# Two expert blocks in plain fp32 instead of four, weights split in halves, tables built inside the whole blocks

## The chip, the cores and the metric

The kernel runs on one core of one Trainium2 chip. The metric is the device time of one execution in microseconds (us). The engines are named as in the profile: PE is the matmul engine, PEld its weight loads, ACT is ScalarE, DVE is VectorE, POOL is GpSimd, SP is SyncE. A name with a q behind it (SPq, ACTq) is that engine's instruction queue, from which transfers are issued.

## The reference

Sixteen images of 5 x 128 x 128 become 16 x 256 tokens of 256 features; then one attention layer with a decay, then a mixture of eight experts of which each token takes two. All of it is fp32.

```
h = layernorm(patches(x) @ W) * gamma                    # tokens: 320 -> 256
xn = layernorm(h)
q, k, v, g = silu(xn Wq), silu(xn Wk), xn Wv, sigmoid(xn Wg)   # 256 -> 1024, 16 heads of 64
cum = cumsum(-softplus(xn Wa + ba))                      # one per head and token
attn = (q k^T) * exp(cum_i - cum_j), causal
h += (groupnorm(attn v) * gn_w + gn_b) * g @ Wo
xf = layernorm(h);  p = softmax(xf Wr);  the two best experts of each token
h += sum over the two of p_e * (gelu(xf W1_e + b1_e) W2_e + b2_e)      # 256 -> 1024 -> 256
```

## The kernel before

**Parts of a product.** Most products are made from fp32 numbers cut in two: ACT copies the number into an fp32r tile (the high part, `*_hi`), DVE subtracts this from the number (the low part, `*_lo`), and PE adds three products, high by high, high by low and low by high (`three`). Some products are made from the plain fp32 numbers, without the cut; PE's records then have two instructions for each product.

**Attention.** It runs over eight pairs of images (p = 0 to 7), each in eight steps (c = 0 to 7), every engine with its own program, written out and ordered by hand; semaphores join them. A step makes queries, keys and gates of two heads, scores and the weighted sum. Ahead of the first step, SP loads the tokens' patches and the four attention weights (`load_weight`, L470), ACT and DVE cut them (`weight_hi` L856, `weight_lo` L1797), a fifth weight (wo) and the token weights (`token_weights_hi`, `token_weights_lo`) are cut within steps 0 and 1. The running sums `cum` go out to memory and come back spread over the partitions (`store_cum`, `load_decay`).

**Routing.** After attention, tokens are normed, their two experts chosen (`choose`, `weigh`, `keep_ranks`, `place` on DVE; `top_exp` on ACT; `route`, `ranks` on PE), and POOL scatters each token's row to its experts' lists (`scatter`).

**Expert blocks.** 256 rows of one expert's list are a block. Blocks 0 to 9 come from the counts of the first five pairs; their experts and places are in the table `tab` before attention ends (`first_tables`, `first_places`). The later blocks' places need the counts of all pairs; `last_tables` (L2022) makes them in 40 small DVE instructions, each of which waits for the one before. Of these, instruction 2 gives the ends of the lists (`padi`), to which SP writes padding (`pad_list`), instructions 39 and 40 write the table of blocks 10 and up.

The first NF = 4 blocks are **early** ones: plain fp32 (`early1`, `early2` on PE, `active_early` on ACT), put between the last steps of attention and of routing. Then come **whole** blocks, cut in parts, 4 to 21, in a loop of two blocks per pass (`whole_row` on PE L1673, ACT L1132, DVE L2298), and behind them **mixed** rounds with blocks of 128 rows. All engines take their work strictly in the order of their programs.

**The order in a whole row for block k.** PE: second half of layer 1 of k, transposes of the rows of k+1 (L1399), first half of layer 2 of k, first half of layer 1 of k+1, second half of layer 2 of k. ACT, for each of eight chunks c: the gelu of chunk c+1 (L964), the high part of the hidden chunk c (L984), and a quarter of the high part of the next block's w1 (c = 0 to 3) or w2 (c = 4 to 7) (L958); after c = 3 the high part of the next rows (L950). DVE, for each c: low part of the hidden chunk (L2123), a quarter of the low part of w1 or w2 (L2114), at c = 2 the block's result before (`keep_y`, L2091), at c = 3 the low part of the next rows, at c = 4 `row_tails`. ACT's first gelu of row k+1 waits for DVE's last hidden chunk of row k; PE's chunk c waits for the gelu four chunks before it (`hidden_free`).

**SP's order.** For each whole block: w1, w2, then b2 of the block before, the rows, b1 (`load_whole`, L586). Before block NF+2 stands `sp.wait_ge(M["tb"], 2)` (L644), before block 10 `sp.wait_ge(M["tb"], 40)` (L652); `tb` counts the table instructions. These lines:

```
            sp.wait_ge(M["tb"], 2)
            for j in range(NF + 2, N1):
                load_whole(whole(j), whole(j - 1))
                for e in range(X // 2):
                    pad_list(X // 2 * (j % 2) + e) if j < NF + 4 else None
            ...
            sp.wait_ge(M["tb"], 40)
            load_whole(whole(N1), whole(N1 - 1))
```

Of the kernel before, what the change touches and what calls it, by code (L numbers as in the profile page):

```python
# [27 lines left out]
P = 128  # L28
# [27 lines left out]
WQ = 4  # L56
YB = (BS + 1) // 2
HB = 4
NF = 4
# [16 lines left out]
def vit_layer(nc, xT, w_tok, gamma, wq, wk, wv, wg, wa, ba, wo, gn_w, gn_b,  # L76
# [3 lines left out]
    with ExitStack() as ctx:  # L80
# [224 lines left out]
        passed mh_done zeroed c_in c_sum ws_in0 ws_in1 ws_in2 ws_in3 ws_hi ws_lo wt_in g_in  # L305
        xt_in0 xt_in1 xt_in2 xt_in xth_done xtl_done wth_done wtl_done tok_ps s1_st s1_u s1_v0 s1_v1 s1_st2 s1_ve s1_rs s1_h s1_xn
        s1_tps s1_xnT s1_aps s1_z h_out sp_step sp_m sp_la gnh
        xh_done xl_done cum_ps cc_done ncum_done ct_ps ct_copied cum_out0 cum_out1
# [47 lines left out]
        def two_whole(q):  # L356

            return (Blk(2 * q, 0, q, 2 * q - NF, 4 * q, 4 * q - 2, q - 1, q - 1),
                    Blk(2 * q + 1, 1, q, 2 * q + 1 - NF, 4 * q + 2, 4 * q, q - 1, q - 1))

# [18 lines left out]
        W_IN = [("ws_in0", 1), ("ws_in1", 1), ("ws_in2", 1), ("ws_in3", 1), ("ws_in1", 2)]  # L379
        w_parts = [wsp[0], wsp[2], wsp[1], wsp[3], wo_sp]  # L380


        @block.sync
        def _(sp):
# [85 lines left out]
            def load_weight(i):  # L470
                have(sp, "ws_lo", 2 if i == 4 else 0)
                sp.dma_start(stage_w[i].rearrange("p (k n) -> p k n", k=EC if i < 4 else NP),
                             W_ATT[i].rearrange("(k p) n -> p k n", p=P)).then_inc(M[W_IN[i][0]], 16)
# [15 lines left out]
            store_h(1)  # L489
            load_weight(4)  # L490
# [7 lines left out]
            for p in range(NPR):  # L498
                for c in range(NP):
# [301 lines left out]
        def _(act):  # L801
            act.dma_start(wt[:, 0:KT, :], w_tok[0:KT * P, :].rearrange("(k p) n -> p k n", p=P)).then_inc(M["wt_in"], 16)
            for at in (0, KREM):
                act.dma_start(wt[at:at + KREM, KT, :], w_tok[KT * P:FEAT, :]).then_inc(M["wt_in"], 16)
            for dst, src in ((gammaB[:, :], gamma.rearrange("(a n) -> a n", a=1).broadcast_to([P, E])),
# [3 lines left out]
                act.dma_start(dst, src).then_inc(M["c_in"], 16)  # L809

# [13 lines left out]
            def token_weights_hi():  # L824
                act.wait_ge(M["wt_in"], 48)
                act.activation(wt_hi, wt[:, :, :], ACT.Copy).then_inc(M["wth_done"], 1)

            def softplus(p):

                act.wait_ge(M["s1_z"], p + 1)  # L830
# [25 lines left out]
            def weight_hi(i):  # L856
                act.wait_ge(M[W_IN[i][0]], 16 * W_IN[i][1])
                act.activation(w_parts[i][0].rearrange("p k n -> p (k n)"), stage_w[i], ACT.Copy).then_inc(M["ws_hi"], 1)
# [11 lines left out]
            def tanh_g(p, c):  # L870
                act.wait_ge(M["g_ps"], NP * p + c + 1)
                if p == 0 and c == GC:
                    act.wait_ge(M["ws_lo"], 5)
# [12 lines left out]
            def decay(p, c, u):  # L886
                n = 2 * NP * p + 2 * c + u
                act.wait_ge(M["causal"], 2 * (n + 1))
                act.wait_ge(M["ncum_done"], p + 1)
# [5 lines left out]
            def keep_o(p, c):  # L895
                act.wait_ge(M["o_ps"], 2 * NP * p + 2 * c + 2)
                have(act, "wo_ps", 4 * (p - 1) + 2 * (c // GC) + 2)
                act.activation(osb[:, c, :], bank[3][:, :], ACT.Copy).then_inc(M["o_done"], 1)
# [109 lines left out]
            def step(p, c):  # L1008
# [20 lines left out]
                if (p, c) == (0, 0):  # L1029
                    token_weights_hi()  # L1030
                if (p, c) == (0, 1):
                    weight_hi(4)
# [1385 lines left out]
```

## Time and profile before

| | |
|---|---|
| median of 3 runs | 1226.39 us (1219.59 to 1227.38) |
| the profiled execution | 1219.53 us, its span 1217.7 us, 1.8 us around it |
| busy share of the span | PE 98%, PEld 87%, ACT 71%, DVE 69%, POOL 35% |
| granted PE clock, mean | 0.997 |

Attention takes the span to about 740 us, the early blocks to about 820 us, whole blocks to about 1040 us, mixed rounds the rest. A row of a timeline gives start, duration, engine, line, operation, tiles and count; in brackets stands the engine's idle time before it and what ended that. Rows of one line and tile that follow each other are merged. A busy PE need not be PE at its peak, since its instructions overlap; the spacing of starts is the safer reading.

### The profile page before, as it was taken

The numbers are of one execution on the slowest core, as the hardware profiler recorded it, in microseconds if no ns is written. First come the engines' busy times: TensorE is split into PE (matmuls) and PEld (weight loads), VectorE is DVE, ScalarE is ACT, GpSimd is POOL, SyncE is SP. The second block draws the span as 40 slices with busy tenths as digits, with TensorE's granted clock in tenths as the row PEclk, the third lists the DMA queues.
The fourth block names the chain that finished last, engine by engine and source line by source line (L and its number), as shares of the span: only waits on it lengthen the run. The fifth ranks groups of instructions, "written<-read, shape, count | busy, mean of one in ns | idle before, by whom it ended". The sixth has DMA issues, their size and how long they took to land. (4 is left out here: it accounts for less than half of the span.)

```text
span 1217.7 us, 27487 instructions
## 1 busy us (share of the span) xinstructions
PE 1198.1 (98%) x8560; PEld 1055.2 (87%) x8560; DVE 844.5 (69%) x2182; ACT 868.7 (71%) x2033; POOL 429.7 (35%) x521
## 2 busy tenths in 40 slices
PE   9999999999999999999999999999999999999997
PEld 6788788788888888888888788889999999999996
DVE  5655676776776776776776677578888888465663
ACT  4767767767767767767767758458888888666663
POOL 2212222242242242242242151555454545443433
PEclk9999999999999999999999999999999999999999
DMA  6532232242242352342342248498988786899984
GB/s 201 180 112 83 91 108 92 89 144 87 94 144 82 99 144 81 100 144 81 100 127 85 95 125 274 144 279 238 266 227 247 218 247 184 238 290 255 277 248 99
DMA packets 126730, 195.39 MB, mean 160 GB/s; under 512 B 16497, under 2 KB 92625, under 8 KB 126481
## 3 DMA queue, kind: packets, MB, share of 16 engines
q1 hardware_dynamic: 111904, 176.22, 45.6%
q0 software_dynamic: 13584, 17.26, 7.2%
q8 instruction: 54, 0.88, 0.3%
q10 hardware_dynamic: 1136, 0.61, 0.2%
q14 instruction: 52, 0.42, 0.1%
HBM read 168.32 MB, written 29.05 MB: 162 GB/s over the span
## 5 line engine op out<-in xcount | busy, mean ns | idle before, releaser
L1276 PE MATMUL bank<-xn_sp,big_r 128*128 128x512 f32 x1152 | 297.1, 400 | 1.4 <-DVE dec_x L1822 0.9
L1276 PEld LDWEIGHTS bank<-xn_sp,big_r 128*128 128x128 f32 x1152 | 208.9, 189 | 48.1 <-issue 1.8
L700 POOL TENSOR_SCALAR_AFFINE_SELECT dec_x<-dec_x 128x256 f32<-128x256 f32 x256 | 112.2, 466 | 355.5 <-DMA dec_x<-cum_scratch 355.0
L893 ACT ACTIVATE dec_x<-dec_x,ncum 128x256 f32<-128x256 f32 (+1 forms) x512 | 186.7, 446 | 11.8 <-POOL dec_x L700 11.8
L1622 PE MATMUL bank<-big_r 128*128 128x256 f32 x1296 | 168.7, 286 | 1.0 <-ACT q_s L964 1.0
L1622 PEld LDWEIGHTS bank<-big_r 128*128 128x128 f32 x1296 | 161.0, 192 | 2.6 <-ACT q_s L964 1.6
L1822 DVE TENSOR_TENSOR dec_x<-bank,dec_x 128x384 f32<-128x384 f32 x256 | 125.5, 549 | 39.3 <-PE bank L1321 34.2
L757 POOL DMA_INDIRECT out<-mid_f,tok x68 | 116.4, 1711 | 63.6 <-DMA out<-mid_f,tok 26.7
L751 POOL TENSOR_SCALAR mid_f<-mid_f,dec_x 128x256 f32<-128x256 f32 x68 | 72.8, 1076 | 155.4 <-DVE mid_f L2091 152.9
L964 ACT ACTIVATE mid_f<-bank,h 128x256 f32<-128x256 f32 x216 | 101.1, 479 | 28.1 <-PE bank L1622 14.8
L2123 DVE TENSOR_TENSOR big_r<-mid_f,big_r 128x256 fp32r<-128x256 f32 x216 | 91.2, 423 | 38.0 <-ACT big_r L984 38.0
L2114 DVE TENSOR_TENSOR big_r<-big_f,big_r 128x512 fp32r<-128x512 f32 x148 | 101.4, 691 | 9.8 <-ACT big_r L958 2.6
L1269 PE MATMUL bank<-big_r,xn_sp 128*128 128x512 f32 x384 | 99.3, 395 | 0.3 <-ACT big_f L875 0.3
L1362 PE MATMUL bank<-big_r,y_sp 128*128 128x256 f32 x512 | 96.8, 284 | 0.0
L958 ACT ACTIVATE big_r<-big_f 128x512 fp32r<-128x512 f32 x148 | 93.7, 637 | 3.9 <-DMA big_f<-in_L_ffn_w 3.9
L984 ACT ACTIVATE big_r<-mid_f 128x256 fp32r<-128x256 f32 x216 | 92.1, 427 | 0.0
L1318 PE MATMUL bank<-q_s,k_s 64*128 64x256 f32 x512 | 83.8, 402 | 3.4 <-issue 3.0
L1634 PE MATMUL bank<-big_r 128*128 128x256 f32 x672 | 86.3, 285 | 0.0
L722 POOL DMA_INDIRECT expert_rows<-xn,slot x64 | 65.1, 1018 | 58.3 <-DVE slot L1965 42.2
L1269 PEld LDWEIGHTS bank<-big_r,xn_sp 128*128 128x128 f32 x384 | 70.7, 188 | 15.5 <-issue 1.4
L1634 PEld LDWEIGHTS bank<-big_r 128*128 128x128 f32 x672 | 82.2, 191 | 0.0
L1362 PEld LDWEIGHTS bank<-big_r,y_sp 128*128 128x128 f32 x512 | 81.2, 191 | 1.0
(257 smaller groups left out, 2327.4 us busy)
## 6 DMA issues: line engine op xcount, KB each, us to landing
big_f<-in_L_ffn_w SPq DMA_DIRECT2D x68, 1024.0 KB, 6.8
dec_x<-cum_scratch SPq DMA_DIRECT2D x128, 384.0 KB, 3.9
big_w<-in_L_ffn_w SPq DMA_DIRECT2D x12, 1024.0 KB, 7.7
mid_f<-expert_rows SPq DMA_DIRECT2D x27, 261.0 KB, 3.1
h_scratch<-h SPq DMA_DIRECT2D x16, 256.0 KB, 2.2
h<-h_scratch SPq DMA_DIRECT2D x8, 512.0 KB, 4.0
out<-h SPq DMA_DIRECT2D x16, 256.0 KB, 4.3
xt<-in_x SPq DMA_DIRECT2D x14, 256.0 KB, 4.3
```

The costliest lines, as they stand in the source:

```text
L700: pool.affine_select(out=d, in_=d, pattern=[[0, 2], [1, P]], compare_op=ALU.is_ge, fill=fill, base=0, channel_multiplier=-1).then_inc(M["c ...
L757: pool.indirect_dma_start(out=out_rows, out_offset=bass.IndirectOffsetOnAxis(ap=tok[k.par][:, s:s + 1], axis=0), in_=yo[k.par][:, s, :], i ...
L893: act.activation(d, d, ACT.Exp, bias=ncum[p % 2][:, NS * u + s, 2 * c + hh:2 * c + hh + 1]).then_inc(M["exp_done"], 1)
L958: act.activation(parts[0].rearrange("p k n -> p (k n)")[:, cols], staged[:, cols], ACT.Copy).then_inc(M[f"{name}_hi"], 1)
L964: act.activation(target, bank[hbank[c % HB]][:, 0:width], ACT.Gelu_apprx_tanh, bias=b1_sb[k.par][:, c:c + 1]).then_inc(M["gel_done"], 1)
L1269: mm = pe.matmul(bank[target][:, :], xp[:, k, t * P:(t + 1) * P], wp[:, k, n * 512:(n + 1) * 512], start=(k == 0 and j == 0), stop=(k == E ...
L1276: mm = pe.matmul(bank[target][:, :], wp[:, k, c * P:(c + 1) * P], xp[:, k, :], start=(k == 0 and j == 0), stop=(k == EC - 1 and j == 2))
L1362: mm = pe.matmul(bank[target][:, s * E:(s + 1) * E], yp[:, j, u * S + s * P:u * S + (s + 1) * P], wp[:, GC * g + j, :], start=(j == 0 and ...
L1622: mm = pe.matmul(bank[hbank[c % HB]][:, 0:BLK], wp[:, i, c * P:(c + 1) * P], xp[:, i, :], start=(i == 0 and j == 0), stop=(i == EC - 1 and ...
L1634: mm = pe.matmul(bank[6][:, s * E:(s + 1) * E], gp[:, c, s * P:(s + 1) * P], wp[:, c, :], start=(c == 0 and s == 0 and j == 0), stop=(c == ...
L1822: dve.tensor_tensor(d, score_bank(p, c, u, hh)[:, 0:LW], d, ALU.mult).then_inc(M["mult_done"], 1)
L2114: dve.tensor_tensor(lo, staged[:, cols], f32(hi), ALU.subtract).then_inc(M[f"{name}_lo"], 1)
```

## The change

NF becomes 2: blocks 2 and 3 become whole blocks. `last_tables` is cut into seven parts, `tables_0` to `tables_6`, which DVE does at c = 5 of the rows of blocks 2 to 8; DVE's first eight whole rows are written out for that. SP's two `tb` waits stay as they are, the first now standing before block 4. Block 2's w1 and rows are cut on ACT ahead of `keep_x2` of the last image, its w2 behind `top_exp` and a wait for the end of early block 1, whose weights lie in the same place. On SP the last two stores of h move ahead of block 2's rows. On DVE `row_tails` of blocks 0 and 1 come a little later. At the start of attention the four weights are loaded and cut in halves by columns, some halves within steps 0 to 2; wo is loaded and cut later; the third image's `embed` comes ahead of step 0; the token weights' low part moves to step 1; the second copy of the token weights' last rows is not waited for at first; PE's filler matmuls at the very start go from 5 to 6. Three semaphores are merged into others.

```diff
-NF = 4
+NF = 2
...
+        PIECES = [(0, 0), (1, 0), (2, 0), (3, 0), (0, 1), (1, 1), (2, 1), (3, 1), (4, 0)]
...
@@ SP
-            sp.wait_ge(M["wt_in"], 48)
+            sp.wait_ge(M["wt_in"], 32)
...
-            load_weight(0)
-            load_weight(1)
-            load_weight(2)
-            load_weight(3)
+            for i, h in PIECES[0:8]:
+                load_weight(i, h)
             store_cum(0)
-            for c in range(2):
-                for u in range(2):
-                    load_decay(0, c, u)
+            for u in range(2):
+                load_decay(0, 0, u)
             store_h(0)
             store_h(1)
-            load_weight(4)
+            for u in range(2):
+                load_decay(0, 1, u)
...
+                    if (p, c) == (0, 0):
+                        load_weight(4, 0)
...
             for j in range(1, NF):
                 load_next_early(j)
-                if j == 1:
-                    sp.wait_ge(M["o_ps"], 2 * NP * NPR)
-                    sp.dma_start(then, then_d.broadcast_to(then.shape)).then_inc(M["tb_in"], 16)
-                if j == 2:
-                    store_h2(NPR - 1, 0)
-                    store_h2(NPR - 1, 1)
+                sp.wait_ge(M["o_ps"], 2 * NP * NPR)
+                sp.dma_start(then, then_d.broadcast_to(then.shape)).then_inc(M["tb_in"], 16)
             weights_whole(whole(NF))
+            store_h2(NPR - 1, 0)
+            store_h2(NPR - 1, 1)
             rows_whole(whole(NF))
             load_whole(whole(NF + 1), whole(NF))
             sp.wait_ge(M["tb"], 2)
@@ ACT
+            weight_hi(1, 1)
+            token_weights_hi()
             decay(0, 0, 0)
             decay(0, 0, 1)
...
             for c in range(4, HC):
                 active_early(1, c)
+            first = whole(NF)
+            for q in range(WQ):
+                w_hi("w1", w1_sp[0], w1_f[0], "w1_in0", 1, "q_ps", NP * NPR, q)
+            act.wait_ge(M["wo_ps"], 4 * NPR)
+            x_hi(first, 0)
             keep_x2(2 * NPR - 1)
-            x_early(2)
             top_exp(2 * NPR - 2)
             top_exp(2 * NPR - 1)
...
             for q in range(WQ):
                 w_hi("w2", w2_sp[0], w2_f[0], "w2_in0", 1, "y_ps", 2, q)
@@ PE
...
             turn_rows(k, rows_f[0], BS)
-            for c in range(4):
-                early2(3, c)
+            early2(1, 0)
+            turn2(2 * NPR - 1, "lg_done", 2 * NPR - 1)
+            early2(1, 1)
+            route(2 * NPR - 1)
+            early2(1, 2)
+            early2(1, 3)
             layer1(k, 0, one)
+            ranks(NPR - 1, "lg_done", 2 * NPR)
             for c in range(4, HC):
-                early2(3, c)
+                early2(1, c)
@@ DVE
-            def last_tables():
+            def tables_0():
...
+            def tables_6():
...
-            row_tails(whole(0), rows_u[0], BS)
             weigh(p - 1)
             place(p - 1, 0)
             place(p - 1, 1)
+            row_tails(whole(0), rows_u[0], BS)
...
-            def whole_row(k, b_par, before, nxt):
+            def whole_row(k, b_par, before, nxt, tables=None):
...
                     if c == 4:
                         row_tails(k, rows_f[k.par], BS)
+                    if c == 5 and tables is not None:
+                        tables()
...
-            with dve.Fori(NF // 2, LAST // 2 - 1) as q:
+            k0, k1, k2 = two_whole(NF // 2) + two_whole(NF // 2 + 1)[0:1]
+            whole_row(k0, 0, two_whole(NF // 2 - 1)[1], k1, tables_0)
+            whole_row(k1, 1, k0, k2, tables_1)
...
+            whole_row(k0, 0, before, k1, tables_6)
+            whole_row(k1, 1, k0, k2)
+            with dve.Fori(NF // 2 + 4, LAST // 2 - 1) as q:
```

## Rows read from the trace of the kernel before

**Rows 1.** The page, part 1: busy time, share of the span and instructions.

```profile
PE 1198.1 (98%) x8560; PEld 1055.2 (87%) x8560; DVE 844.5 (69%) x2182; ACT 868.7 (71%) x2033; POOL 429.7 (35%) x521
```

**Rows 2.** Timeline of PE: transposes that open early block 3, whole block 4, two later rows.

```profile
796.36 0.60 PE L1399 MATMUL bank<-ident,wt 128*128 128x128 f32 x4
...
810.61 0.60 PE L1399 MATMUL bank<-ident,mid_f 128*128 128x128 f32 x4
...
871.49 0.60 PE L1399 MATMUL bank<-ident,mid_f 128*128 128x128 f32 x4
...
883.43 0.60 PE L1399 MATMUL bank<-ident,mid_f 128*128 128x128 f32 x4
```

**Rows 3.** Timeline of PE between early blocks 1 and 2: its two waits for routing.

```profile
779.06 0.66 PE L1373 MATMUL bank<-ident,xn 128*128 128x128 f32 x4 [0.45 <-DVE lg L1901]
...
784.61 0.38 PE L1390 MATMUL bank<-both,strict 128*128 128x32 f32 x2 [0.97 <-DVE upto L1934]
```

**Rows 4.** Timeline of ACT in a whole row: first two gelus, hidden chunk, w1, next rows.

```profile
877.61 0.84 ACT L964 ACTIVATE mid_f<-bank,h 128x256 f32<-128x256 f32 x2 [0.66 <-DVE big_r L2123]
878.34 0.42 ACT L984 ACTIVATE big_r<-mid_f 128x256 fp32r<-128x256 f32 x1
878.65 0.63 ACT L958 ACTIVATE big_r<-big_f 128x512 fp32r<-128x512 f32 x1
...
883.93 0.66 ACT L950 ACTIVATE big_r<-bank 128x256 fp32r<-128x256 f32 x2 [1.08 <-PE bank L1399]
```

**Rows 5.** Timeline of DVE in a whole row: chunk 6, a quarter of w2, chunk 7.

```profile
876.09 0.42 DVE L2123 TENSOR_TENSOR big_r<-mid_f,big_r 128x256 fp32r<-128x256 f32 x1
876.42 0.69 DVE L2114 TENSOR_TENSOR y_sp<-big_f,y_sp 128x512 fp32r<-128x512 f32 x1
877.02 0.42 DVE L2123 TENSOR_TENSOR big_r<-mid_f,big_r 128x256 fp32r<-128x256 f32 x1
```

**Rows 6.** Timeline of DVE: table instructions 1, 2, 32 and 40 of 40.

```profile
793.71 0.16 DVE L2026 SCALAR_TENSOR_TENSOR dec_x<-iota,taken 128x8 f32<-128x8 f32 x1
793.90 0.17 DVE L2027 CAST padi<-dec_x 128x8 int32<-128x8 f32 x1
...
802.13 0.17 DVE L2061 TENSOR_SCALAR dec_x<-dec_x 128x9 f32<-128x9 f32 x1
...
804.02 0.18 DVE L2069 CAST tab<-dec_x 128x30 int32<-128x30 f32 x1
```

**Rows 7.** Timeline of SP's queue: four paddings and the w1 behind them.

```profile
829.81 4.54 SPq L631 DMA_DIRECT2D expert_rows<-in_c_pad  x4
835.45 0.39 SPq L423 DMA_DIRECT2D big_f<-in_L_ffn_w  x1
```

**Rows 8.** DMA issues, 740 to 900 us: count, size, median us from issue to landing.

```profile
big_f<-in_L_ffn_w SPq DMA_DIRECT2D x18, 1024.0 KB, 6.5
...
h<-in_L_ffn_b SPq DMA_DIRECT2D x12, 4.0 KB, 3.7
```

**Rows 9.** Timeline of ACT: table load, four gelus; four quarters of block 4's w2.

```profile
787.09 1.28 ACT L964 ACT_TABLE_LOAD   x1 [3.63 <-issue]
788.39 1.80 ACT L964 ACTIVATE q_s<-bank,h 128x256 f32<-128x256 f32 x4
...
811.77 2.20 ACT L958 ACTIVATE big_r<-big_f 128x512 fp32r<-128x512 f32 x4
```

**Rows 10.** Groups by line, ACT, whole run: count | busy us, mean ns | idle before.

```profile
L964 ACT ACT_TABLE_LOAD x3 | 3.8, 1283 | 3.7 <-issue 3.6
```

**Rows 11.** Timeline of PE in steps 0 and 1 of attention: decay products, two waits.

```profile
41.35 0.65 PE L1334 MATMUL bank<-dec_x,mid_f 128*64 128x256 f32 x4
...
44.23 0.70 PE L1318 MATMUL bank<-q_s,k_s 64*128 64x256 f32 x4 [1.35 <-issue]
...
48.29 1.61 PE L1276 MATMUL bank<-xn_sp,big_r 128*128 128x512 f32 x6 [0.89 <-DVE dec_x L1822]
```

**Rows 12.** Windows: us, busy of PE, PEld, DVE, ACT, POOL (count), PE clock, DMA share, GB/s.

```profile
24.00:26.00 2.00, 2.00 (x6) 1.10 (x5) 1.61 (x2) 1.97 (x3) 0.00 (x0) 0.50 0.00 0
```

More of the change, by code:

```diff
@@ L1046, in step @@
                 tanh_k(p, c + 1)
+                if p == 0 and c < 3:
+                    weight_hi(*((2, 1), (3, 1), (4, 0))[c])
                 if c == 0 and p > 0:
@@ L1071, in step @@
                     scaled_h(2 * p + 2)
-            weight_hi(0)
-            weight_hi(1)
+            weight_hi(0, 0)
+            weight_hi(1, 0)
             keep_xnT(0)
@@ L1082, in _ @@
             keep_cum(0)
-            weight_hi(3)
-            for i in range(1, TP):
-                keep_v(0, i, 2 + i)
+            weight_hi(3, 0)
+            keep_v(0, 1, 3)
+            scaled_h(0)
+            keep_v(0, 2, 4)
+            keep_v(0, 3, 5)
+            scaled_h(1)
             tanh_k(0, 0)
+            weight_hi(0, 1)
             tanh_g(0, 0)
-            scaled_h(0)
-            scaled_h(1)
+            weight_hi(1, 1)
+            token_weights_hi()
             decay(0, 0, 0)
@@ L1113, in _ @@
                 active_early(1, c)
+            first = whole(NF)
[3 more added lines that the diff above has]
+            x_hi(first, 0)
             keep_x2(2 * NPR - 1)
-            x_early(2)
             top_exp(2 * NPR - 2)
             top_exp(2 * NPR - 1)
-            for c in range(HC):
-                active_early(2, c)
-            x_early(3)
-            first = whole(NF)
-            for c in range(HC):
-                active_early(3, c)
-                if c == 3:
-                    for q in range(WQ):
-                        w_hi("w1", w1_sp[0], w1_f[0], "w1_in0", 1, "q_ps", NP * NPR, q)
-            act.wait_ge(M["wo_ps"], 4 * NPR)
-            x_hi(first, 0)
             for q in range(WQ):
@@ L1289, in keys @@
             def keys(p, c):
-                if p == 0 and c == 0:
-                    pe.wait_ge(M["ws_lo"], 3)
+                if p == 0 and c in (0, NP // 2):
+                    pe.wait_ge(M["ws_lo"], weight_done(2, c // (NP // 2)))
                 have(pe, "sk_done", NP * p + c)
@@ L2176, in step @@
                     keep_logits(2 * p - 2)
-                if c == 1 and nxt:
+                if c == 1 and nxt and p > 0:
                     patches_lo(2 * p + 3)
@@ L2201, in step @@
                         affine(2 * p - 1)
-                    if nxt:
+                    if nxt and p > 0:
                         embed(2 * p + 2)
@@ L2242, in _ @@
             silu_q(0, 0)
-            weight_lo(2)
-            weight_lo(3)
+            weight_lo(3, 0)
             silu_k(0, 0)
+            weight_lo(0, 1)
+            embed(2)
             dve.wait_ge(M["g_in"], 16 * 7)
@@ L2252, in _ @@
                     step(p, c)
-                    if p == 0 and c == 1:
-                        weight_lo(4)
+                    if p == 0 and c == 2:
+                        weight_lo(4, 0)
             p = NPR - 1
@@ L2279, in _ @@
             choose(2 * p)
+            for q in range(WQ):
+                w_lo("w1", w1_sp[0], w1_f[0], 0, q)
+            x_lo(whole(NF), 0)
             keep_logits(2 * p + 1)
             choose(2 * p + 1)
+            row_tails(whole(1), rows_u[1], BS)
             weigh(p)
-            row_tails(whole(1), rows_u[1], BS)
             keep_ranks(p)
```

162 lines of the change are left out of this document (80 added, 82 removed).

## The prediction

> **What bounds the kernel now.** I read the page first: PE is busy for 98% of the span, so only PE's path can shorten it [rows 1]. Then PE's timeline in the expert stage, by starts and not by busy time. An early block goes from the transposes at 796.36 to those at 810.61: 14.25 us. A whole block goes from 871.49 to 883.43: 11.94 us, and all whole rows keep that pace [rows 2]. Then I asked how much room the other engines have inside a whole row. ACT waits 1.08 us for PE's transposes before it makes the high part of the next rows [rows 4]; its other wait, 0.66 us, is for DVE's last hidden chunk. DVE and ACT thus form a ring: ACT's first gelu of a row waits for DVE's chunk 7 of the row before, and DVE's chunks wait for ACT. The ring's own pace is about 11.94 - 1.08 = 10.9 us, so its room is about 1.0 us per row. What is put on DVE between chunk 5 and chunk 7 lengthens the ring directly.
>
> **PE's work.** Two early blocks become whole ones: 2 x (14.25 - 11.94) = **4.6 us less** [rows 2].
>
> **The end of routing.** Before, PE waits 0.45 + 0.97 us there [rows 3]. After, ACT puts four quarters of w1 (2.20 us, as four quarters of w2 took) and the two row copies (0.66 us) ahead of `keep_x2` of the last image [rows 4, 9]; `route` of that image needs it. Counting PE's work from the end of early block 1's layer 1, it reaches `route` about 1.5 us before ACT is done. One wait takes the other's place: **0**. The two stores of h, now ahead of block 2's rows on SP, hold these rows back until the last residual; by the order of PE's work two microseconds of cover are left.
>
> **The entry to the whole rows.** ACT's cut of block 2's w2 waits for the last matmul of early block 1, and all of ACT's gelus of block 2 stand behind it. Four quarters take 2.20 us; then a table load, since the function before was an exp: 1.28 us; then the first gelu, 0.48 us [rows 4, 9]. PE's chunk 4 of layer 1 needs that gelu: 4.0 us. The second comes 0.36 us later, the third and fourth each 1.19 us after it (gelu, hidden chunk, quarter of w1 by their starts [rows 4]), so the fourth is ready at 6.7 us and PE's last chunk ends 7.45 us after the early block. A row is sixteen chunk products and 0.44 us of transposes, so one is (11.94 - 0.44) / 16 = 0.72 us; without the wait these four would end at 2.9 us. **4.6 us more.** Ends: 2.5 us if the load falls into ACT's earlier idle time and PE only waits for quarters and gelu; 5.6 us if the ring, which starts with no lead, costs one more microsecond in the next row.
>
> Here the table load itself can be disputed. In the row the load takes 1.28 us and the gelu begins 0.02 us behind it (787.09 + 1.28 to 788.39) [rows 9]. The Trainium skill, page "ScalarE: Activation LUTs", section "What ACT_TABLE_LOAD costs", puts a drain of about 1.38 us on top of 1.28 us for each switch; by it this term would be 6.0 us. The trace shows no such drain, so I keep the row.
>
> **Two waits of SP on the tables.** This is the largest part. Before, the tables were ready while early block 2 ran, long before SP needed them. After, `tb >= 2` stands before block 4's w1 and becomes true in row 2 at c = 5. The second table instruction starts 0.19 us after the first and takes 0.17 us [rows 6]: 0.4 us. SP then needs a register load and an issue; between the last padding's end (829.81 + 4.54) and the next w1's issue lie 1.1 us [rows 7]. The transfer lands 6.5 us after issue, the median of 18 [rows 8]. Together 8.0 us from the start of `tables_0`. ACT wants that w1 behind the first two gelus and the first hidden chunk of row 3: `tables_0` itself (1.24 us to instruction 6), then chunk 6, a quarter of w2, chunk 7 (0.33 + 0.60 + 0.42 us [rows 5]) and 878.65 - 877.61 = 1.04 us on ACT [rows 4]: 3.7 us. ACT stands for 4.3 us with its remaining gelus behind, and PE, without a lead after the entry, stands as long: **4.3 us more**. Queued behind the wait on SP are w2, b2, the rows and b1 of block 4; they follow within 2 us and are not needed earlier than w1's successors.
>
> `tb >= 40` stands before block 10's w1 and becomes true at the end of `tables_6` in row 8; ACT wants it in row 9. From that end: 1.1 + 6.5 = 7.6 us against 1.35 + 1.04 = 2.4 us. **5.2 us more.** Both depend on the landing: at 3.7 us, which a 4 KB transfer takes [rows 8], they would be 1.5 and 2.4 us; each microsecond of landing above 6.5 us adds one to both.
>
> **The tables.** Instruction 1 starts at 793.71, the fortieth ends at 804.20: 10.5 us in seven parts of 1.1 to 2.3 us [rows 6]. Before they ran beside plain fp32 matmuls; DVE had no chunk to deliver. Now each part stands between chunk 5 and chunk 6, in the ring. Seven rows have 7 x 1.0 us of room: **3.5 us more**. Ends: 0, if PE's lead covers all; 10.5 us if the room is not there.
>
> **Table loads in the loop.** No gelu load appears behind 787.09, three in all [rows 9, 10]: both loops were entered with the gelu's table in place. After, ACT's loop is entered behind an exp but closed behind a gelu. A load that serves the first pass sits in the loop's body and then comes in every pass, 1.28 us for two rows. In rows 4, 6 and 8 the room is already spent: 3 x 1.28 = **3.8 us more**; later 1.28 us against 2.0 us of room cost nothing. Ends: 0, if it is placed ahead of the loop, and 9 x 1.28 = 11.5 us.
>
> **The start.** The first decay product (41.35) hangs on `cum`, its way through memory and ACT's exp, which moves little: `cum` now stands behind the first value product, and two decay loads, not four, come first. Behind it PE loses 1.35 + 0.89 us [rows 11]; the token weights' low part and an `embed` leave DVE there, half weights come in. The eight half loads cost SP four more issues, long before `store_cum`; ACT's new waits for low parts in steps 1 and 4 come behind halves that DVE makes a step earlier. I take **1.0 us less**; ends: 2.2 us less with both waits gone, 0.6 us more with `cum` later.
>
> **Sum.** -4.6 + 0 + 4.6 + 4.3 + 5.2 + 3.5 + 3.8 - 1.0 = **+15.8 us**. Attention and the mixed rounds stay. Against the profiled execution: 1219.53 + 15.8 = 1235.3; against the median, which stands 6.9 us above it: 1242.2. The four executions shown stand two by each, so I say 1240.
>
> **Rivals.**
> *The load is placed once, ahead of the loop*: +12.0 us, 1232 to 1238. For it: no pass of either loop before had one. Against it: these were entered with the right table.
>
> *PE's clock falls in the stalls.* PE stands for 4 to 5 us three times, longer than any wait in the trace of before. From 24 to 26 us the granted clock is 0.50, the 1.2 GHz level, behind a stretch of small matmuls and a short wait [rows 12]. The Trainium skill, page "TensorE: Matmul & The Clock Gate", Part 1, says that an idle PE goes to the lower of two clocks and needs sustained work to return. Each fall would cost up to a quarter row at half clock, 2.9 us: +15.8 and up to 8.7 us; I price it at +21 us, 1243 to 1250.
>
> *Not slower: the weights of blocks 4 and 10 arrive in time.* The place is ACT's first quarter of w1 in rows 3 and 9. It decides at a landing below 2.2 us for block 4 (3.7 - 1.5) and 1.3 us for block 10, or if the ring's lead over PE is several microseconds, as it is not in [rows 4]. Then, with loads hidden as well: -4.6 + 4.6 + 3.5 - 1.0 = +2.5 us, 1222 to 1229. No transfer in [rows 8] is that quick.
>
> *Only the plain exchange counts*: -4.6 - 2.2 us and the entry hidden, 1213 to 1220; it needs every added wait to be covered.
>
> **Chances.** Forecast 0.45; load once 0.20; clock 0.16; weights in time 0.13; plain exchange 0.06. One per cent, 12.3 us, is about what this kernel's measurement can tell from no change. Slower by more: most of the forecast, under half of the second, all of the third: 0.60. Within: 0.35. Faster: 0.05. The range, 1222 to 1254, takes in the landing's ends, the clock and the third rival's lower part; the likeliest's own is 1233 to 1247.
>
> **What would show it.** After: whole rows at 11.94 us except rows 2, 3 and 4 to 9; PE waits of 4 to 5 us before layer 1 in rows 2, 3 and 9, released by ACT; ACT waiting 4 to 5 us for the transfer of `in_L_ffn_w` twice; about eleven table loads at L964 where there were three. Wrong would be: no such transfer waits, PE at 11.94 us through rows 3 to 9, or a total under 1222 us.

## The result, and the profile after

The changed kernel takes **1250.97 us**, median of 4 runs (1247.61 to 1253.56), against 1226.89 us for the kernel before in 4 runs (1219.59 to 1229.18): a ratio of 1.0204, 95% interval 1.0169 to 1.0238. It is slower by 2%. Its profiled execution took 1249.19 us with a span of 1247.3 us; that of before took 1219.53 us. The profiles thus lie 29.7 us apart and the medians 24.1 us: the runs of before spread over some 13 us, most of them near 1220 or near 1228 us, and its profile is one of the former (experiments 7 to 9).

Where the 29.6 us between the two spans arise, by the starts of the same transposes and decay products in both timelines of PE:

| stretch | before, up to | after, up to | added | forecast |
|---|---|---|---|---|
| attention, to its last step's decay products | 741.81 | 746.39 | +4.6 | -1.0 |
| to the transposes of block 4 | 810.61 | 826.12 | +10.9 | +6.0 |
| rows 4 to 8, to block 9 | 871.49 | 892.11 | +5.1 | +5.1 |
| rows 9 and 10, to block 11 | 895.38 | 925.40 | +9.4 | +5.7 |
| to the last whole row | 1038.74 | 1072.13 | +3.4 | 0 |
| mixed rounds, to the end | 1217.7 | 1247.3 | -3.8 | 0 |

Row k is here and below the time from the transposes of block k to those of block k+1. The forecast column splits the prediction's terms: of the 4.6 us of PE's work 3.4 lie ahead of block 4's transposes and 1.2 in row 4; of the seven parts of the tables, 0.5 us each, one lies ahead of these transposes, five in rows 4 to 8, one in row 9. The last row of the table is no effect of the change that could be told from scatter: over the fourteen profiled executions of this document the stretch takes 175.0 to 179.2 us, and before (179.0) and after (175.2) lie near the two ends.

PE's waits first. The lines are timeline rows of PE in the changed kernel; its code has shifted, so layer 1 is L1608 there, layer 2 L1620, the transposes L1409, early layer 2 L1457, the first decay product L1344.

```profile
43.09 1.12 PE L1344 MATMUL bank<-dec_x,mid_f 128*64 128x256 f32 x4 [4.62 <-DVE dec_x L1813]
...
73.18 1.61 PE L1286 MATMUL bank<-xn_sp,big_r 128*128 128x512 f32 x6 [1.67 <-DVE dec_x L1813]
...
786.39 2.07 PE L1457 MATMUL bank<-big_w,q_s 128*128 128x256 f32 x4 [2.80 <-DVE mid_f L2098]
...
803.87 5.49 PE L1608 MATMUL bank<-big_r 128*128 128x256 f32 x24 [4.12 <-ACT mid_f L980]
809.16 1.03 PE L1409 MATMUL bank<-ident,mid_f 128*128 128x128 f32 x4
...
821.52 0.98 PE L1608 MATMUL bank<-big_r 128*128 128x256 f32 x6 [1.26 <-ACT mid_f L980]
...
826.12 0.65 PE L1409 MATMUL bank<-ident,mid_f 128*128 128x128 f32 x4 [2.44 <-DMA mid_f<-expert_rows]
826.53 4.61 PE L1620 MATMUL bank<-y_sp,big_r 128*128 128x256 f32 x24
...
907.34 0.98 PE L1608 MATMUL bank<-big_r 128*128 128x256 f32 x6 [3.38 <-ACT mid_f L980]
...
911.45 1.11 PE L1409 MATMUL bank<-ident,mid_f 128*128 128x128 f32 x4 [1.66 <-DMA mid_f<-expert_rows]
912.21 4.71 PE L1620 MATMUL bank<-y_sp,big_r 128*128 128x256 f32 x24
```

Before, no wait in these stretches was longer than 1.35 us [rows 3, 11]. Now look at the durations behind the long ones: 24 products of layer 1 take 5.49 us and of layer 2 4.61 and 4.71 us, where 24 in an undisturbed stretch take 3.04 to 3.22 us. The windows (same columns as [rows 12]) say why:

```profile
43.00:45.00 2.00, 1.91 (x12) 1.34 (x14) 1.28 (x4) 1.28 (x2) 0.00 (x0) 0.50 0.02 4
...
786.00:788.00 2.00, 1.61 (x4) 1.34 (x5) 1.86 (x12) 0.34 (x2) 1.45 (x2) 0.53 1.07 375
...
803.87:809.16 5.29, 5.29 (x25) 5.29 (x25) 4.36 (x9) 4.70 (x12) 4.07 (x5) 0.50 0.33 121
809.87:812.90 3.03, 3.03 (x26) 3.03 (x25) 2.43 (x9) 3.01 (x9) 2.16 (x3) 0.97 0.13 47
...
828.00:830.00 2.00, 2.00 (x11) 2.00 (x11) 1.80 (x8) 2.00 (x7) 1.69 (x1) 0.50 0.96 307
...
912.00:914.00 2.00, 2.00 (x11) 2.00 (x10) 1.09 (x3) 1.75 (x5) 1.25 (x2) 0.50 1.02 389
916.00:918.00 2.00, 2.00 (x19) 2.00 (x19) 2.00 (x6) 1.37 (x4) 1.55 (x1) 1.00 0.99 193
```

The granted clock is 0.50, the 1.2 GHz level, behind the waits before 43.09, 786.39, 803.87, 826.12 and 911.45, and 1.00 again some microseconds later. In the windows behind the waits column 2 shows PE busy all the time: a busy share would not show this slowness. How much of it is lost in the total is a question of its own (experiments 2 and 4).

Third, the table loads and ACT's waits, the answers to [rows 9, 10] (group by line, then ACT's timeline at the entry and in rows 3 and 9):

```profile
L980 ACT ACT_TABLE_LOAD x11 | 14.1, 1283 | 10.4 <-DVE big_r L2130 10.3
```

```profile
799.85 2.19 ACT L974 ACTIVATE big_r<-big_f 128x512 fp32r<-128x512 f32 x4 [7.15 <-PE bank L1457]
802.05 1.28 ACT L980 ACT_TABLE_LOAD   x1
803.35 0.84 ACT L980 ACTIVATE mid_f<-bank,h 128x256 f32<-128x256 f32 x2
...
820.48 0.63 ACT L974 ACTIVATE big_r<-big_f 128x512 fp32r<-128x512 f32 x1 [2.40 <-DMA big_f<-in_L_ffn_w]
...
906.30 0.63 ACT L974 ACTIVATE big_r<-big_f 128x512 fp32r<-128x512 f32 x1 [3.99 <-DMA big_f<-in_L_ffn_w]
```

Eleven loads, as forecast: two for the early blocks and one in each of the nine passes of the loop. The Trainium skill, page "ScalarE activation tables: per-element evaluation and per-set limits", section "Table sets in the compiler and the runtime", says that loads are placed per block of code; the count agrees. The load starts 0.01 us behind the last quarter of w2 (799.85 + 2.19), and the first gelu 0.02 us behind the end of the load (802.05 + 1.28), so the drain that the prediction weighed does not appear in this trace either.

### The profile page after: what moved, and what is told of

It is laid out like the page before. It is cut to its first block and busy times, and to the rows that moved or that the text cites. A ratio compares the mean times of both kernels' runs of the same rounds, so it can differ in the third digit from the quotient of the medians.

```text
span 1247.3 us, 27691 instructions
## 1 busy us (share of the span) xinstructions
PE 1205.3 (97%) x8626; PEld 1062.9 (85%) x8626; DVE 861.0 (69%) x2222; ACT 891.5 (71%) x2077; POOL 433.9 (35%) x521
## 5 line engine op out<-in xcount | busy, mean ns | idle before, releaser
L1608 PE MATMUL bank<-big_r 128*128 128x256 f32 x1392 | 184.4, 289 | 10.3 <-ACT mid_f L980 10.3
L1608 PEld LDWEIGHTS bank<-big_r 128*128 128x128 f32 x1392 | 175.2, 194 | 13.3 <-ACT mid_f L980 12.2
L763 POOL TENSOR_SCALAR mid_f<-mid_f,dec_x 128x256 f32<-128x256 f32 x68 | 77.6, 1146 | 178.0 <-DVE mid_f L2098 172.6
L2130 DVE TENSOR_TENSOR big_r<-mid_f,big_r 128x256 fp32r<-128x256 f32 x232 | 98.1, 423 | 49.6 <-ACT big_r L1000 49.2
L980 ACT ACTIVATE mid_f<-bank,h 128x256 f32<-128x256 f32 x232 | 108.7, 480 | 30.1 <-PE bank L1608 16.2
L2121 DVE TENSOR_TENSOR big_r<-big_f,big_r 128x512 fp32r<-128x512 f32 x160 | 110.2, 693 | 17.3 <-ACT big_r L974 9.7
L974 ACT ACTIVATE big_r<-big_f 128x512 fp32r<-128x512 f32 x160 | 101.0, 635 | 15.7 <-DMA big_f<-in_L_ffn_w 8.6
L1000 ACT ACTIVATE big_r<-mid_f 128x256 fp32r<-128x256 f32 x232 | 99.3, 429 | 0.0
L1620 PE MATMUL bank<-big_r 128*128 128x256 f32 x720 | 92.7, 285 | 4.7 <-DVE mid_f L2098 4.7
L1620 PEld LDWEIGHTS bank<-big_r 128*128 128x128 f32 x720 | 88.3, 192 | 6.4 <-issue 6.4
L1620 PE MATMUL bank<-y_sp,big_r 128*128 128x256 f32 x672 | 89.6, 291 | 0.0
L1344 PE MATMUL bank<-dec_x,mid_f 128*64 128x256 f32 x512 | 81.5, 397 | 4.6 <-DVE dec_x L1813 4.6
```

The costliest lines, as they stand in the source:

```text
L974: act.activation(parts[0].rearrange("p k n -> p (k n)")[:, cols], staged[:, cols], ACT.Copy).then_inc(M[f"{name}_hi"], 1)
L980: act.activation(target, bank[hbank[c % HB]][:, 0:width], ACT.Gelu_apprx_tanh, bias=b1_sb[k.par][:, c:c + 1]).then_inc(M["gel_done"], 1)
L1000: act.activation(g_sp[0][:, c, :], gel[c % NGEL], ACT.Copy).then_inc(M["gh_done"], 1)
L1608: mm = pe.matmul(bank[hbank[c % HB]][:, 0:BLK], wp[:, i, c * P:(c + 1) * P], xp[:, i, :], start=(i == 0 and j == 0), stop=(i == EC - 1 and ...
L1620: mm = pe.matmul(bank[6][:, s * E:(s + 1) * E], gp[:, c, s * P:(s + 1) * P], wp[:, c, :], start=(c == 0 and s == 0 and j == 0), stop=(c == ...
L2121: dve.tensor_tensor(lo, staged[:, cols], f32(hi), ALU.subtract).then_inc(M[f"{name}_lo"], 1)
```

## The experiments

Experiments 1 to 6 start from the changed kernel; four runs each, and the differences are to the median of its four runs above, which were taken at another time. The kernel before, run beside them and beside the changed kernel, had medians of 1225.3 to 1226.9 us, so differences under some 2 us say little.

**1. The loop's table loads.** One gelu in ACT's idle time ahead of the loop:

```
             top_exp(2 * NPR - 1)
+            act.activation(za[:, 0:8], za[:, 0:8], ACT.Gelu_apprx_tanh)
             for q in range(WQ):
```

> The changed kernel, with one gelu of 8 columns on a tile that is no longer read, put on ACT between the last exp and the cut of block 2's second weight, where ACT waits 7.15 us anyway. Theory (the load in the loop is on the path): one load of 1.28 us comes there and none later; the entry wait of 4.12 us falls to about 2.8, two rows of the loop go from 24.74 us back to about 23.9, rows 4, 6 and 8 get up to 0.5 us shorter each; total 5 to 7 us less. Rival (the loads are covered by the rows' room, the tables and the weights set the pace): only the entry's 1.3 us come back, total 1 to 2 us less.

Measured: 1242.25 us (1241.6 to 1242.98), 8.7 us below the changed kernel's median. The load stands alone in idle time, and two remain at L980:

```profile
L980 ACT ACT_TABLE_LOAD x2 | 2.6, 1283 | 0.0
...
L1140 ACT ACT_TABLE_LOAD x1 | 1.3, 1283 | 0.0
```

All rows of the loop from block 11 on take 11.94 to 11.95 us; in the changed kernel every second one took 12.79. Rows 5 to 8 take 11.96 + 12.40 + 13.14 + 12.25 = 49.75 us, in the changed kernel 12.77 + 13.57 + 13.13 + 13.02 = 52.49: two loads, 1.4 us each. Row 4 takes 13.49 us without its load and 13.50 with it: there the load cost nothing that shows. The entry wait is 2.70 us. The theory holds: its 5 to 7 us fit the two profiled executions, which differ by 7.1 us, and are short by the medians.

**2. SP's wait on the tables, each place by itself.** First, for block 4:

```
-            sp.wait_ge(M["tb"], 2)
             for j in range(NF + 2, N1):
                 load_whole(whole(j), whole(j - 1))
+                if j == NF + 2:
+                    sp.wait_ge(M["tb"], 2)
```

> The changed kernel, with SP's wait for the second table instruction moved behind the loads of block 4, to the paddings that need it. Theory (the wait holds the weights and the rows): block 4's first weight is there when ACT wants it, PE's waits in row 3 (1.26 + 0.21 us before layer 1, 2.44 us before the transposes) go, and the half clock behind them; the time from the transposes of block 3 to those of block 4 falls from 16.96 us to 12 to 13, the total by 4 to 6 us. Rival (the ring has no lead, row 4 takes it back): row 3 gets shorter and rows 4 and 5 longer, total under 2 us less.

Measured: 1246.23 us, 4.7 us less. The time from block 3's to block 4's transposes is 12.96 us, the only wait of PE left there is 0.21 us, and rows 4 and 5 take 13.90 and 13.14 us, 0.8 more together than in the changed kernel: the ring takes back little. Row 4 is no shorter although its first layer 2 now takes 3.12 us and not 4.61: there the half clock cost nothing that shows. Then for block 10:

```
-            whole_row(k1, 1, k0, k2, tables_5)
+            whole_row(k1, 1, k0, k2, lambda: (tables_5(), tables_6()))
...
-            whole_row(k0, 0, before, k1, tables_6)
+            whole_row(k0, 0, before, k1)
```

> The changed kernel, with the last two parts of the tables both in row 7, none in row 8. Theory (the wait holds block 10's weight and rows): tables are ready near 888 us, PE's waits of 3.38 + 0.21 + 1.66 us in row 9 go and the half clock behind them; row 9 falls from 19.34 us to 12 to 13, row 10 from 13.95 to 12 to 12.5, row 7 gets 0 to 2 us longer, row 8 as much shorter; total 7 to 9 us less. Rival (the tables in the ring cost what they take): row 7 gets over 2 us longer, and total is 4 to 6 us less.

Measured: 1245.82 us, 5.2 us less, below the range. Row 9 falls from 19.34 to 13.14 us and row 10 from 13.95 to 11.95, 8.2 us together, but the double part lengthens row 8 from 13.02 to 14.96: the rival's price, paid beside the theory's gain. Row 11 takes 12.77 us in place of 11.94, since the loop's table load there is no longer hidden behind the long wait. (What the code of row 7 does on DVE falls into the time counted here as row 8.)

**3. Both waits, and the tables a row earlier.** `tables_0` goes into DVE's idle 2.12 us ahead of block 2's second weight, each later part one row forward:

```
             place(p, 1)
+            tables_0()
             for q in range(WQ):
                 w_lo("w2", w2_sp[0], w2_f[0], 0, q)
```

> The changed kernel, with the first part of the tables ahead of the low part of block 2's second weight, where DVE waits 2.12 us, and each later part one row earlier; the last is in row 7. Theory (SP's two waits on the tables are the cause): both become true in time, block 4's and block 10's weights and rows are there; rows 3 and 9 take 12 to 13.2 us in place of 16.96 and 19.34, row 10 12 in place of 13.95; total 10 to 13 us less, which is the sum of the two single changes (4.7 and 5.2) and the double part's cost. Rival (DVE's order at the entry): the part delays layer 2 of row 2 by 1.3 us, rows 3 and 4 keep it, total 6 to 9 us less.

Measured: 1240.11 us (1239.01 to 1240.78), 10.9 us less; ratio to before 1.0115 (1.0071 to 1.016). Row 3 takes 13.67 us, row 9 13.15 and row 10 11.94; the entry's wait stays at 4.12 us, so the part there is hidden. The two waits on the tables, with the half clock behind them and this one part, are worth 11 us.

**4. The clock by itself.** Sixteen products that nobody reads fill PE's wait at the entry; no other engine gets anything earlier:

```
                 early2(1, c)
+            pe.wait_ge(M["taken_done"], NPR)
+            for i in range(16):
+                pe.matmul(bank[7][:, 0:P], ones[:, :], ident[:, :], start=True, stop=True)
```

> The changed kernel, with sixteen products of two constant 128x128 tiles (about 3.4 us, their sum is not read) put on PE behind early block 1, where PE waits 4.12 us for the first gelu of block 2. Nothing comes earlier on any engine. Theory (the clock falls in the wait): the granted clock stays at 1.00, the four chunks behind take 3.0 to 3.7 us in place of 5.49, set by ACT's gelus at most; the transposes of block 3 come 1.5 to 2.5 us earlier and the total is 1 to 2.5 us less. Rival (the four chunks are slow because ACT's gelus come at 1.19 us each): they take 5 us or more as before, total the same.

Timeline of PE and two windows (the fill, the four chunks):

```profile
797.56 3.73 PE L1665 MATMUL bank<-ident,ones 128*128 128x128 f32 x32
801.85 2.53 PE L1608 MATMUL bank<-big_r 128*128 128x256 f32 x18 [0.56 <-ACT mid_f L980]
...
805.40 0.60 PE L1409 MATMUL bank<-ident,mid_f 128*128 128x128 f32 x4
...
821.20 2.84 PE L1608 MATMUL bank<-big_r 128*128 128x256 f32 x12 [3.04 <-ACT mid_f L980]
```

```profile
797.56:801.29 3.73, 3.73 (x33) 3.54 (x31) 2.56 (x4) 3.45 (x5) 3.10 (x3) 1.00 0.20 72
801.85:805.40 3.55, 3.34 (x24) 3.07 (x25) 2.62 (x6) 3.55 (x10) 2.64 (x4) 1.00 0.31 112
```

The clock stays at 1.00 and the four chunks take 3.55 us, not 5.29. From the end of early block 1 to the transposes it is 805.40 - 797.56 = 7.84 us against 809.16 - 799.75 = 9.41: 1.6 us, as expected. But the total is 1249.96 us, 1.0 us less and within the scatter of the runs: in row 3 PE, earlier now, waits 3.04 us for the weight of block 4 in place of 1.26. The clock's cost in this stretch is shown, 1.6 us, and also that a gain ahead of a gate ends at the gate.

**5. The entry.** ACT's gelus of chunks 0 to 3 go ahead of the cut of block 2's second weight:

```
             top_exp(2 * NPR - 1)
+            for c in range(NGEL):
+                activated(first, c)
             for q in range(WQ):
```

> The changed kernel, with ACT's first four gelus of block 2 ahead of the cut of its second weight, in the 7.15 us in which ACT waits for early block 1; ACT's first two whole rows stand ahead of its loop. Theory (ACT's order makes the entry): PE does not wait before chunk 4 (4.12 us in the changed kernel), the four chunks take 2.9 to 3.0 us in place of 5.49, layer 2 behind them may wait up to 1 us for the second weight's low part; no gelu load comes in the loop. The transposes of block 3 come 5 to 6 us earlier against the end of early block 1, the total is 9 to 12 us less, of which 5 are the loop's loads. Rival (the cut of the second weight is the limit): PE waits 3 to 4 us before layer 2 instead, and the total is 5 to 7 us less.

Measured: 1244.84 us, 6.1 us less, and the rival is right. PE runs chunks 4 to 7 at once and then stands before layer 2:

```profile
797.81 3.23 PE L1614 MATMUL bank<-big_r 128*128 128x256 f32 x24
800.87 0.60 PE L1415 MATMUL bank<-ident,mid_f 128*128 128x128 f32 x4
805.15 4.62 PE L1626 MATMUL bank<-big_r 128*128 128x256 f32 x24 [3.68 <-DVE mid_f L2104]
```

It waits for the sum of early block 1, which DVE keeps behind four low parts of a weight and three hidden chunks. The clock falls behind this wait as well (0.63 over these 4.62 us). The 6.1 us are not the entry's: this kernel's loop has no table loads either (three at L980 in all), which alone was worth 8.7 us in experiment 1, and block 4's transposes come at 823.61 us, there at 822.81.

**6. The start.** The embedding of image 2, which waits on DVE 4.30 us for the store of h, returns behind the decays:

```
             weight_lo(0, 1)
-            embed(2)
```

> The changed kernel, with the embedding of image 2 put back to its old place on DVE, behind the first decay products' preparation. Theory (order on DVE): it waits 4.30 us for the store of h and the decays' multiplication stands behind it; at its old place the wait of 4.62 us before the first decay product falls below 1 us, that product starts at 38.5 to 40 us in place of 43.09, PE does not run at half clock behind it, and the total falls by 4 to 7 us. Rival (the way through memory): the decay rows arrive too late anyway, the product starts at 42 us or later and the total falls by under 1 us.

Measured: 1252.04 us, no gain. The product at 43.09 comes at 41.35 with a wait of 1.09 us, but the next one is 2.02 us at 48.63, and the decay product of step 1 starts where it did (56.33 against 56.27). So the embedding did cause the first wait, and the wait moved to the next step. In this execution PE also ran at a granted clock of 0.53 and 0.62 from 22 to 26 us, which makes its first sums 1.7 us later (26.52 against 24.78); the median has no gain either. Moving the output weight's low part behind step 3's decays as well:

```
                 decayed(p, c, 1)
+                if (p, c) == (0, 3):
+                    weight_lo(4, 0)
```

> The changed kernel, with the embedding of image 2 back at its old place on DVE (as before, which left the second decay product where it was), and the low part of the output weight (2.29 us on DVE) moved behind the decays' multiplication of step 3. Theory (each piece of DVE's work ahead of the decays is a wait of PE): the wait of 1.67 us near 73 us goes, the first one stays short; the first decay product of step 3 (77.88) comes 1.3 to 3 us earlier, the total is 1.5 to 3 us less than the changed kernel's. Rival (the next wait takes its place): the low part is waited for at the next step, the total stays within 1 us.

Measured: 1250.81 us, no gain. The wait of 1.67 us before 73.18 became one of 1.85 us on ACT's tile at 74.16; ACT itself stands 2.98 us there, for a low part of a weight on DVE, and step 3's first decay product comes at 79.11, not ahead of 77.88. Here the rival holds. In the experiment before it only the rival's total came: its product was to start at 42 us or later and started at 41.35.

**7. The start alone**, with all of the expert part as before:

> The kernel before with the start of the change alone: halves of the attention weights, the order of the first sums and values, the second part of the token weights' load; four early blocks and the old tables. Theory (the start loses): the first decay product waits 3.9 to 5.7 us and a second wait of 1.7 us follows, as in the changed kernel, and the total is 2 to 4 us above the kernel before. Rival (my forecast of the start): 0 to 1 us less than before.

Measured in 12 runs: 1223.75 us (1220.89 to 1226.26) against 1227.41 us in 29 runs of before; ratio 0.9988, interval 0.9963 to 1.0013. Both fail in part. The trace has the theory's waits:

```profile
44.06 0.65 PE L1353 MATMUL bank<-dec_x,mid_f 128*64 128x256 f32 x4 [4.59 <-DVE dec_x L1841]
```

The first decay product is 2.7 us later than in [rows 11], the last step 4.7 us. Yet the median is below that of before, though the interval takes in no difference. The runs explain it: those of before lie mostly near 1220 or near 1228 us, up to 1231.7; none of the new start is above 1226.3. Something in the old start costs some 8 us in 18 of the 29 runs (those above 1225 us), and the start of the change has it removed while it adds its own 5 (1224.44 - 1219.53 between the profiled executions). By these medians the expert part of the change, on its own start, costs 1250.97 - 1223.75 = 27.2 us.

**8. All corrections together**, once on the old start, once on the new:

> The kernel before with its own start and the change's expert part (two early blocks, tables in parts), and four corrections: the first part of the tables ahead of block 2's second weight and each later part a row earlier; ACT's first four gelus of block 2 ahead of that weight's cut; on DVE the sums of early blocks 0 and 1 kept before the work that waits for scatters and weights; on PE early block 1's layer 2 finished ahead of block 2's layer 1. Theory (all lost time sat in single waits): the gain of PE's work, 4.6 us, comes out less 2 to 3 us for the tables in the ring and about 1 us at the entry; no wait of PE over 2 us after 60 us; total 1222 to 1226 us, up to 4 us less than before. Rival (a further wait takes their place): 1228 us or more.

> The same four corrections on the changed kernel, thus with its own start, in which the embedding of image 2 and the output weight's low part stand behind the decays' multiplication. Theory: 2 to 4 us more than with the old start, 1225 to 1229 us. Rival (the start is worth what was forecast): 0 to 1 us less than with the old start.

Measured: 1233.24 us (ratio 1.0045, 1.0016 to 1.0074) on the old start and 1230.92 us (1.0041, 1.0017 to 1.0065) on the new. On the old start the rival is right; on the new one neither holds, since it is 2.3 us less than with the old, outside both. 18 and 20 of the 24 us are back, but not all: against the start alone (experiment 7) the corrected expert part still costs 1230.92 - 1223.75 = 7.2 us, so the 4.6 us of PE's work do not come out as a gain. In the kernel with the new start, rows 4 to 9 take 79.3 us where before's pace gives 13.09 + 5 x 11.95 = 72.8, with PE waiting up to 0.94 us at a time for DVE. At the entry DVE now has the ranks, the first tables and the kept sum ahead of the weight's low part, PE waits 3.48 us before layer 2, and half clock follows (0.63 over 4.64 us):

```profile
804.03 4.64 PE L1626 MATMUL bank<-big_r 128*128 128x256 f32 x24 [3.48 <-DVE big_r L2136]
```

The times of the one with the old start are again apart (1225 to 1228 and 1233 to 1235 us), and its profiled execution, 1234.32 us, is of the longer ones. It shows what was sought, in PE's timeline and one window:

```profile
1.29 4.58 PE L1195 MATMUL bank<-dec_x 128*128 128x256 f32 x10 [1.29 <-DVE dec_x L2223]
7.62 5.07 PE L1214 MATMUL bank<-wt,xt 128*128 128x256 f32 x12 [1.75 <-DMA wt<-in_L_tok_W]
```

```profile
10.00:22.00 12.00, 12.00 (x25) 7.04 (x24) 5.45 (x16) 3.82 (x2) 1.25 (x2) 0.50 0.90 346
```

PE's warm-up ends, the token weights are not there, PE waits 1.75 us, and from 10 us on the token products run at the 1.2 GHz level; the first decay product comes at 48.04 us.

**9. The first ten microseconds alone**, in the kernel before:

```
-            keep_running(5)
-            pe.wait_ge(M["wt_in"], 48)
+            keep_running(6)
+            pe.wait_ge(M["wt_in"], 32)
```

and the second copy of the token weights' last rows is loaded behind the constants; SP's wait for the token weights goes from 48 to 32 as well.

> The kernel before with only the first ten microseconds of the changed start: six warm-up groups on PE in place of five, and the second copy of the token weights' last rows loaded after the constants, so that PE waits for two loads and not for three. Theory (what the changed start gains lies there): PE reaches the token products without a wait of 0.9 to 1.75 us, the granted clock stays at 1.00 up to 22 us, the first decay product keeps its place near 41 us in place of 44; the times of 1226 to 1232 us that the kernel before shows in half its runs go, and the median is 1219 to 1222 us, 0.4 to 0.6% below before. Rival (the gain lies in the halves of the attention weights and the earlier sums): median 1225 to 1228 us, no different from before.

Measured in 12 runs: **1219.16 us** (1216.96 to 1220.44) against 1224.64 us in 17 runs of before (1216.54 to 1232.15); ratio 0.9957, interval 0.9928 to 0.9987. No run is above 1220.5 us, PE goes on without a gap, and the clock holds:

```profile
1.29 5.49 PE L1199 MATMUL bank<-dec_x 128*128 128x256 f32 x12 [1.29 <-DVE dec_x L2230]
6.57 3.75 PE L1218 MATMUL bank<-wt,xt 128*128 128x256 f32 x12
```

```profile
10.00:22.00 12.00, 12.00 (x59) 8.31 (x57) 9.07 (x20) 6.32 (x6) 2.16 (x2) 1.00 0.86 324
```

This is the one kernel here that is faster than before, by 0.4%. Which of its edits does it was not tried apart. Nor is half clock shown to be the whole of it: no long run of before was profiled, and of the runs of before near 1228 us some have a mean granted clock of 0.988 to 0.993, others 0.998.

## Why the prediction was right, and where its sizes were off

The direction and most of the mechanisms are as forecast; the sum was +15.8 us and the medians say +24.1. Part of the number's fit is luck. Against the profile from which the sum was made it is +29.6 us, nearly twice; 1250.97 us lies outside the 1233 to 1247 us of the likeliest case and just above the clock rival's 1243 to 1250. The wide range to 1254 holds it.

- **Table loads and tables: nearly right.** Eleven loads were forecast and came. In rows 5 to 8 the tables alone cost 49.75 - 4 x 11.95 = 1.95 us (forecast 0.5 us a row, 2.0) and each of two loads 1.4 us (forecast 1.28). The third load, in row 4, cost nothing that shows (experiment 1), so 2.7 of the 3.8 us came.
- **Loads in later passes: the step "1.28 us against 2.0 us of room cost nothing" failed.** Four passes cost 0.85 us each, 3.4 us. A load falls in one row of two, and PE's layer 2 waits 0.58 us for the sum that DVE keeps behind its third hidden chunk. Room may not be added up over two rows.
- **The two waits on the tables: right in place, short in size.** 4.3 + 5.2 = 9.5 us were forecast, and 10.9 us went when both were removed. The weight came 820.48 - 815.21 = 5.3 us behind its issue, sooner than the 6.5 taken, and ACT waited 2.40 us for it, not 4.3, and 3.99 us for block 10's, not 5.2. PE's waits before layer 1 were to be 4 to 5 us; in row 2 it was 4.12, in row 3 1.26, in row 9 3.38. But that the rows follow within 2 us and are not needed earlier was wrong: they were issued 818.56 - 815.21 = 3.35 us behind the weight and landed 826.12 - 818.56 = 7.6 us after that, and PE waited 2.44 and 1.66 us more for them. In the trace of before such rows land 3.5 us after their issue (median of nine, 740 to 900 us); that the two weights of 1 MB ahead of them make the difference is likely and was not tried apart.
- **The entry: the wait right, the chunks wrong.** 4.0 us were forecast and 4.12 measured. The four chunks were to end 7.45 us behind the early block and ended at 9.41; with the clock held they ended at 7.84. What failed is the step that let them run at full speed, for 1.6 of the 2.0 us that were missing.
- **PE's clock falls in the stalls: this rival, at 0.16, happened beside the forecast.** Set beside the same products at full clock, PE's products in five stretches at 0.50 take longer by about 2.5 us at the start, 1.3 behind 786.39, 2.4 at the entry, 1.5 and 1.6 in layer 2 behind the late rows of blocks 4 and 10: 9.3 us, near the 8.7 at which the rival was priced. These are longer products and not yet lost time. The one stretch that was tested gave back 1.6 of its 2.4 us, and no more than 1.0 us in the total (experiment 4); row 4 was no shorter without its half clock (experiment 2); and the 1.5 and 1.6 us lie within the 10.9 us of the two waits. So the rival's mechanism is shown and its price in the total is not. The page "TensorE: Matmul & The Clock Gate" of the Trainium skill, Part 1, has the same rule, that an idle PE falls to the lower clock and activity releases it. These five rows agree with it; the 12 us of continuous token products in experiment 8 that stay at 0.50 do not, and there the measurement decides. I had the clock as an alternative; it can come on top of every long stall that was forecast, and belonged in the sum's upper end.
- **The end of routing: zero was wrong.** PE waits 2.80 us for a sum that stands on DVE behind a norm which waits 7.19 us for POOL's scatter; [rows 3] had 1.42. In eight other kernels with this order (experiments 1 to 6) the wait was 1.35 to 1.96 us; the clock stayed at 1.00 in five of them and fell to 0.50 in three, so the size varies by execution. The prediction looked at ACT alone there.
- **The start: -1.0 us was forecast on the way, and +4.6 came.** DVE's embedding ahead of the decays was named among the moves but not that it waits for the store of h. That wait is the longest but not the largest part: at the next step's decay product only 1.3 us of the 4.6 have come up (56.27 against 54.93), 1.9 us come behind the wait at 73.18 (77.88 against 74.61 at step 3), the rest later in attention. Against the median of before the start loses nothing (experiment 7, interval 0.9963 to 1.0013), because the old start's long runs go. The sum was made against a profile that is not one of these.
- **Mixed rounds: 0 was forecast, and the 3.8 us are within the scatter** of the profiled executions (175.0 to 179.2 us). Part of it is a wait of PE near the second round, up to 2.0 us, that some executions have and others, the changed kernel's among them, do not. Its cause is open.
- **PE's work, -4.6 us,** was not isolated by any run.

## What to carry to other kernels

Price a stall of PE with the half-clock stretch behind it, as an upper end, and give everything queued behind a waiting transfer its own landing time. Before a stall's removal is credited, name the next gate: in experiments 4 to 6 and 8 the next wait took back part of the gain or all of it. And where the runs of a kernel lie 8 us apart, find out which of them the profile is from before a sum is made against it.

## What the hardware showed that was not expected

Among PE's waits of 0.9 to 2.0 us the length decided little by itself. At 785 us, before the same products, the clock stayed at 1.00 behind waits of 1.35, 1.56, 1.63, 1.76 and 1.96 us and fell to 0.50 behind 1.85, 1.87 and 1.88 us (experiments 1 to 6). Two of them, the second decay experiment and the one with the tables a row earlier, each with its wait and one window:

```profile
786.05 1.13 PE L1457 MATMUL bank<-big_w,q_s 128*128 128x256 f32 x4 [1.96 <-DVE mid_f L2098]
788.00:790.00 2.00, 2.00 (x15) 1.70 (x14) 2.00 (x6) 1.97 (x5) 1.10 (x2) 1.00 0.90 283
...
786.35 1.49 PE L1457 MATMUL bank<-big_w,q_s 128*128 128x256 f32 x4 [1.87 <-DVE mid_f L2098]
788.00:790.00 2.00, 2.00 (x8) 1.73 (x7) 2.00 (x6) 1.25 (x2) 1.10 (x2) 0.50 0.95 303
```

Behind 1.75 us at 7.62 us it fell to 0.50 and stayed there for 12 us of continuous token products. A wait of 0.88 us at the same place in the profile of before left it at 1.00:

```profile
6.80 3.44 PE L1217 MATMUL bank<-wt,xt 128*128 128x256 f32 x12 [0.88 <-DMA wt<-in_L_tok_W]
...
10.00:22.00 12.00, 12.00 (x60) 8.39 (x58) 9.15 (x20) 6.41 (x6) 2.16 (x2) 1.00 0.91 346
```

One more group of warm-up products, under 1 us of PE's time, together with one load fewer to wait for, was worth 5.5 us in the median (1224.64 - 1219.16).
